# The dense attention products of the second layer stand one batch later in each group of eight

## The reference, cut to what matters

```python
# graph attention (8 heads of 64): one message per edge, summed per target node
e = s_src[src] + s_tgt[tgt]; e = where(e >= 0, e, 0.2 * e)
ex = exp(e - m[tgt]);  out = segment_sum(h[src] * alpha[:, :, None], tgt)
# linear attention (8 heads of 32), dense over all nodes
q = elu(xn @ Wq.T) + 1;  k = elu(k) + 1          # k, v = xn @ Wkv.T
context = einsum('bhnd,bhne->bhde', k, v)        # and k.sum over the nodes
attn = einsum('bhnd,bhde->bhne', q, context) * D_inv
```

## Time and profile before

| | us |
|---|---|
| median of three timed runs | 2128.86 |
| span of the profiled execution (no other time of it is listed) | 2334.4 |
| PE busy in it | 2035.6 (87%) |
| DVE, POOL, ACT busy in it | 1287.5, 1033.4, 783.0 |
| mean granted TensorE clock | 0.932 |

### The profile page before, as it was taken

One profiled execution on the slowest core, in us unless ns is written; L12 is line 12 of the kernel. 1 busy time (PEld: TensorE's weight loads), 2 busy tenths in 40 slices (PEclk: granted clock), 3 DMA queues, 4 the chain that ended last, 5 costly groups with the idle time before them and its releaser, 6 DMA issues. The chain is left out here.

```text
span 2334.4 us, 29468 instructions
## 1 busy us (share of the span) xinstructions
PE 2035.6 (87%) x8898; PEld 1313.2 (56%) x8898; DVE 1287.5 (55%) x2800; ACT 783.0 (34%) x2025; POOL 1033.4 (44%) x1084
## 2 busy tenths in 40 slices
PE   7999967888888888599785888888888989999999
PEld 3456633434444446499643566566666955565565
DVE  7696635666766665433365677777677832112121
ACT  4322222222222313243345454445442333322322
POOL 5687855666666540333266566556554410000000
PEclk9999978999999998699897899999889989999999
DMA  4158432322323321622247676667663300000000
GB/s 129 40 108 123 119 105 79 86 84 84 90 83 91 82 64 46 219 73 72 75 145 207 185 208 194 185 195 202 186 183 98 109 1 1 9 10 1 9 10 8
DMA packets 116242, 233.21 MB, mean 100 GB/s; under 512 B 26975, under 2 KB 71142, under 8 KB 113398
## 3 DMA queue, kind: packets, MB, share of 16 engines
q0 software_dynamic: 53168, 151.69, 23.5%
q1 hardware_dynamic: 62918, 79.64, 12.3%
HBM read 190.44 MB, written 40.67 MB: 99 GB/s over the span
## 5 line engine op out<-in xcount | busy, mean ns | idle before, releaser
L2634 PE MATMUL p_ag<-rows_g,oh_g 128*128 128x260 f32 x1408 | 394.8, 429 | 86.5 <-issue 43.7
L2271 POOL DMA_INDIRECT rows_g<-g_table,row_src x352 | 334.7, 951 | 234.7 <-issue 92.1
L948 POOL DMA_INDIRECT rows<-h_table,row_rel x352 | 337.7, 959 | 214.0 <-issue 89.4
L2634 PEld LDWEIGHTS p_ag<-rows_g,oh_g 128*128 128x128 f32 x1408 | 266.6, 207 | 182.4 <-issue 94.7
L3001 DVE SCALAR_TENSOR_TENSOR x<-p_yf,cw_f,x 128x256 f32<-128x256 f32 (+1 forms) x160 | 66.4, 477 | 281.3 <-PE p_yf L3161 281.3
L2385 DVE TENSOR_TENSOR rows_g<-rows_g,p_e 128x2048 f32<-128x2048 f32 x88 | 200.1, 2274 | 3.9 <-issue 3.9
L1280 PE MATMUL p_agg<-rows,oh 128*128 128x256 f32 x704 | 192.1, 414 | 1.9 <-issue 1.8
L402 POOL DMA_INDIRECT slot_table<-rec_f,dst_i x120 | 164.6, 1372 | 39.4 <-issue 39.4
L1073 DVE TENSOR_TENSOR fT<-a_sb,p_sel 128x512 f32<-128x512 f32 x200 | 128.5, 682 | 92.2 <-DMA xT_table<-xT 47.1
L1280 PEld LDWEIGHTS p_agg<-rows,oh 128*128 128x128 f32 x704 | 136.0, 204 | 62.1 <-issue 42.1
L3161 PE MATMUL p_yf<-f,h_f 128*128 128x256 f32 (+1 forms) x640 | 148.4, 386 | 0.8 <-ACT h_f L3053 0.8
(11 more groups left out here) (517 smaller groups left out, 3542.4 us busy)
## 6 DMA issues: line engine op xcount, KB each, us to landing
h_table<-h_out SPq DMA_DIRECT2D x20, 1024.0 KB
where_g<-d_table SPq DMA_DIRECT2D x88, 128.0 KB
w<-in_L_ffn_W SPq DMA_DIRECT2D x16, 512.0 KB, 9.6
y_table<-yb_g SPq DMA_DIRECT2D x47, 128.0 KB, 1.7
rows<-h_table,row_rel POOLq DMA_INDIRECT x352
rows_g<-g_table,row_src POOLq DMA_INDIRECT x352
g_table<-row SPq DMA_DIRECT2D x20, 260.0 KB
f<-in_L_ffn_W SPq DMA_DIRECT2D x16, 256.0 KB, 7.2
```

Of the source, the lines that this page charges most:

```text
L948: pool.indirect_dma_start(rows[:, r, j], None, st.h_rows, bass.IndirectOffsetOnAxis(ap=st.row_rel[:, at:at + 1], axis=0)).then_inc(gathere ...
L2271: pool.indirect_dma_start(rows[:, r, j], None, st.g_table, bass.IndirectOffsetOnAxis(ap=st.row_src[:, at:at + 1], axis=0)).then_inc(gather ...
L2634: last = pe.matmul(p_a[:, k % NS, h, 0:HALF], oh[:, r, j], rows[:, r, j, h * HALF:(h + 1) * HALF], start=j % w == 0, stop=j % w == w - 1)
```

## The change

Four constants of `attend` are each raised by one. Nothing is added or taken away.

```diff
     SPAN = 8
-    KV_AT, Q_AT, CONTEXT_AT = (0, 2), 4, 6
+    KV_AT, Q_AT, CONTEXT_AT = (1, 3), 5, 7
     assert T // 2 * SPAN < NBATCH - NR
```

## The result

The changed kernel takes 2143.34 us (four runs, 2140.27 to 2145.20) against 2128.14 us (four runs, 2124.54 to 2131.22): ratio 1.0075, 95% interval 1.0057 to 1.0092, slower by 15.2 us. The forecast was 2140.5 us.

A forecast was written before the change was run, and what follows sets the result against it. The prediction took a PE and DVE chain from batch to batch as the bound. Ten query terms of +0.45 us and nine key-value terms of +0.79 made +11.6 us: 2140.5 us, slower, range 2108 to 2156.

The forecast's parts named there:

- The bound: Changed stage: a chain through PE and DVE from batch to batch bounds it, 40.98 us per group of eight.
- late words: First profile: DVE and POOL learned late that PE's units were done; POOL idled 2.07 us before one gather; cause not named.
- the estimate from shares of idle time: Changed stage: 48% of its 153 us of idle and half-clock PE taken off 561 us, leaving about 490 us.
- The floor of the gathers: POOL: 32 gathers per group, one every 1.26 us, 40.2 us, just under the chain's 40.98.
- Wide batches: Wide four-column batches receiving a product: +1.72 us for a key-value product, +1.76 us for a query product.
- Narrow batches: Batches losing a product: the four-unit one 1.31 us shorter (query), the two-unit one 0.93 us shorter (key-value).
- Context, "wide to wide: 0": Context product going from phase 6 to 7, both wide batches: no cost, 0 us.
- the query term: Query product from four-unit to wide batch: 1.31 us go, 1.76 come, +0.45 us per group, counted ten times.
- Group 0, key-value "0": Start of stage: PE waits for gathers in batches 0 and 1, so the +0.79 us key-value term counts nine times, not ten.
- rival (b): Batch 5 of each of ten groups gets a half-clock stretch of 1.7 us: 2158 us; chance 9%.
- (a): Rival: the pace of POOL's gathers, with some late words, hides the cost in batches 0 to 3: 2130 us; chance 27%.
- (c): Rival: the change cures the stall of four-unit batches like batch 28 (14.2 us), 18 us faster: 2111 us; chance 22%.

The follow-up runs named there:

- Run 1: The kernel before, no edit, profiled a second time: 2126.47 us, ratio 1.000.
- runs 6 and 7: The kernel before with query products of four-unit batches behind columns 2 and 3 (2112.13 us), or behind columns 1 and 2 (2108.59 us).
- run 5: The kernel before with only the context products moved, from phase 6 to 7: 2130.18 us, ratio 1.0033.
- Run 2: The kernel before with only query products (4 to 5) and context products (6 to 7) moved one batch later: 2141.98 us, ratio 1.0074.
- run 3: The changed kernel with ten idle products, results unread, on PE at the end of each four-unit batch: 2131.21 us, ratio 1.0025.
- runs 3 and 4: Ten idle PE products ending each four-unit batch, added to the changed kernel (2131.21 us) and to the kernel of Run 2 (2127.63 us).
- runs 6 to 10: The kernel before with query products, in two of them key-value products too, one or two columns later inside their narrow batches: 2108.59 to 2112.13 us.

## Why the prediction was right, and where it was not

- **The bound.** Right. From a disturbed profile the prediction chose a path through PE and DVE without late words. Run 1 shows it: no late words, 41.2 us per group (forecast 40.98). The stage was guessed at 490 us and takes 457.3, so the estimate from shares of idle time was 33 us too high; the sum didn't use it. The floor of the gathers was given as 40.2 us, though 32 x 1.26 is 40.3; by the median distance it is 40.0.
- **Wide batches.** +1.72 us for key-value is +1.71, and +1.76 for query is +1.72.
- **Narrow batches.** -1.31 us is -1.22, -0.93 is -0.85. Right, with the reason for the four-unit ones shown by runs 6 and 7: the part ahead of unit 1's end.
- **Context, "wide to wide: 0".** This step failed. In batch 6 the product was hidden beside `query_features`, and without the other moves it costs about 1.0 us per group at full clock (run 5). In the changed kernel two more moves undo it: `query_features` goes to round 7 with the context product (batches 6 and 7: 9.06 us before, 8.80 after), and the key-value product goes out of batch 0, so that the wait for the context sum is gone. Run 2 without the key-value move has that wait, 0.41 us. I had also booked the 0.34 us of `key_features` under the query term, though it moves with key-value. So the sum per group was right (+1.10 for +1.24) and its split was not: query and context +1.0, key-value on top of them +0.1, where I had +0.45 and +0.79. That the errors cancel is luck: the changed kernel happens to move everything that the context product depended on.
- **Group 0, key-value "0".** It failed too. The wait covered the product in batch 0, where it stood before, but not in batch 1, where it went: 3.4 us more in the two batches, of which 1.2 are a longer batch 0 that the trace of run 3 doesn't show (11.90 and 7.52 us).
- **The clock.** I made it rival (b) at 9% with ten stretches of 1.7 us. The price is right (1.68), the count was between: half clock behind four-unit batches in eight of ten groups, in four before. PE's idle time there grew as forecast (2.39 to 2.76 us for 2.6 to 3.1). Run 3 shows that 11 to 12 us of the changed kernel hang on half clock, but the kernel before has some too.
- **The total.** 11.6 us were forecast and 15.2 measured. The stages of the two traces differ by 20.9, and the sum had only the path of it: 11.2 for the 9.9 us of groups 1 to 9, 0.45 for the 3.9 of group 0 and nothing for half clock (7.1). So it is partly luck that the time came out near: the path was a little too large, and the kernel before, by its medians and clocks, probably has more half clock in most executions than in its trace. How the 3.6 us that the forecast lacked divide between clock and group 0 stays open.
- **Rivals.** (a) needed late words or gathers as the bound; neither is there before the change (a group takes 41.2 us, the gathers need 40.0). (c) rested on the 14.2 us batches, which are in no other trace (it counts six groups with them, the first profile has seven).

## What to carry to other kernels

Before work is moved out of a batch that looks long, find what its follower waits for last: here only the work ahead of the end of the second unit was on the path. The query product moved a column or two back inside the same batch gave 14 to 17 us, until the gathers were the bound; query and context products moved to neighbours cost 15. A move that is priced alone can be wrong in company: a product was free only because an addition for another product kept DVE longer in the same round. Work that fills PE's idle time also holds its clock up, even work that nobody needs (runs 3 and 4). A profiled span 10% above the timed runs is to be taken again before its waits are explained.

## What the runs showed of the hardware

In the first profile DVE and POOL went on up to 4 us after the end of the PE instructions that they wait for: DVE's addition of batch 27's unit began at 1433.39, and PE's last column of it (from 1428.10) ended at 1429.22 (the earlier trace rows show the same wait). That was one execution of a kernel that showed nothing of it in the next (spans 2334.4 and 2121.8 us).

How often half clock followed a four-unit batch, by the time for which PE stood still at its end, ten groups in each trace:

| PE idle, us | traces | followed by half clock |
|---|---|---|
| 0.4 to 0.8 | runs 3 and 4 | 0 of 20 |
| 1.3 to 1.8 | runs 6 to 10 | 0 of 50 |
| 2.4 (two of 2.7) | before (run 1), run 5 | 4 and 5 of 10 |
| 2.8 | changed kernel | 8 of 10 |
| 3.1 | run 2 | 7 of 10 |

The same idle time of 2.39 us was followed by either clock, so its length alone doesn't decide.

POOL's indirect gathers start at a median distance of 1.251 us in every trace but the first (1.253).
